# Cross-attention on one core: the key table's products first in slot 0, their rotation first on GpSimd, the mean row in slot 3

## The reference

```
kv_in = concatenate([context_hidden, draft_hidden], axis=1)      # 1601 + 256 rows per batch
q = rope(rms_norm((draft_hidden @ Wq.T) ...))                     # 16 heads of 128
k = rope(rms_norm((kv_in @ Wk.T) ...)); v = kv_in @ Wv.T          # 4 key heads, each used by 4 query heads
attn = softmax(q @ k.T * SCALE) @ v;  x = x + attn @ Wo.T
# for attention 1:
kv_c = kv @ W_kvc;  k_rope = rope(kv_c @ W_kr)                    # the "key table", 64 + 64 columns
# a query looks at the keys from its seg_id - 8 to its seg_id
```

## Time and profile before

| | us |
|---|---|
| three runs | 1948.34, 1949.68, 1951.16 (median 1949.68) |
| the profiled execution's own time | 1947.32 |
| its span | 1945.4 |
| span: TensorE matmul busy | 1723.2 (89%) |
| span: DVE / ACT / GpSimd busy | 1457.1 / 1087.0 / 1122.0 |

### The profile page before, as it was taken

How to read it: one execution, slowest core, us unless ns; L and a number is a source line. 1 busy time by engine, 2 the same in 40 slices (tenths; PEclk the granted TensorE clock), 3 DMA queues, 4 the chain that set the end, 5 groups by cost and what they waited for, 6 DMA issues and landing times. The chain is left out here.

```text
span 1945.4 us, 41606 instructions
## 1 busy us (share of the span) xinstructions
PE 1723.2 (89%) x14578; PEld 1314.0 (68%) x14727; DVE 1457.1 (75%) x3802; ACT 1087.0 (56%) x2676; POOL 1122.0 (58%) x1727
## 2 busy tenths in 40 slices
PE   4789898998998999999999899996999999089997
PEld 2578777787777777777778777775555555038974
DVE  7887896877978778788687787865757765675746
ACT  3567667676667666666766666663133333073543
POOL 5686686775857769568576685600256664072210
PEclk7899999999999999999999999996999999586998
DMA  4121110111110102101011100014368896510100
GB/s 137 46 75 40 34 33 12 40 64 37 50 35 9 34 8 95 43 12 44 1 38 49 54 22 12 8 51 185 117 209 269 270 268 191 161 31 16 45 11 26
DMA packets 74777, 140.25 MB, mean 72 GB/s; under 512 B 11177, under 2 KB 45970, under 8 KB 74322
## 3 DMA queue, kind: packets, MB, share of 16 engines
q1 hardware_dynamic: 64594, 107.21, 17.9%
q0 software_dynamic: 9984, 30.42, 4.4%
HBM read 111.73 MB, written 25.86 MB: 71 GB/s over the span
## 5 line engine op out<-in xcount | busy, mean ns | idle before, releaser
L897 DVE TENSOR_TENSOR att_pT<-att_pT 128x512 bf16<-128x512 f32 (+1 forms) x512 | 319.3, 649 | 156.8 <-ACT att_pT L764 153.6
L552 PE MATMUL att_out<-att_V,att_pT 128*128 128x128 bf16 x5760 | 390.8, 220 | 31.9 <-DVE att_pT L897 24.1
L552 PEld LDWEIGHTS att_out<-att_V,att_pT 128*128 128x128 bf16 x5760 | 351.1, 98 | 63.3 <-DVE att_pT L897 23.3
L764 ACT ACTIVATE att_pT<-att_pT 128x512 bf16<-128x512 f32 (+1 forms) x512 | 277.4, 569 | 172.4 <-PE att_pT L540 171.5
L770 ACT ACTIVATE att_prob<-att_scores,att_negmax 128x512 f32<-128x512 f32 (+1 forms) x512 | 330.1, 654 | 36.4 <-DVE att_negmax L886 34.8
L531 PE MATMUL att_scores<-att_K,att_Q 128*128 128x512 bf16 (+1 forms) x1408 | 299.1, 359 | 8.2 <-DVE att_K L859 1.4
L884 DVE TENSOR_REDUCE att_mx<-att_scores 128x1 f32<-128x512 f32 (+1 forms) x512 | 291.1, 628 | 0.6 <-PE att_scores L531 0.6
L540 PE MATMUL att_pT<-att_ident,att_prob 128*128 128x128 f32 x1920 | 276.5, 275 | 0.0
L531 PEld LDWEIGHTS att_scores<-att_K,att_Q 128*128 128x128 bf16 x1536 | 150.7, 98 | 145.3 <-issue 2.6
L453 PE MATMUL att_aux<-att_wkv,att_kvT 128*128 128x256 bf16 x1440 | 185.7, 280 | 36.9 <-DVE att_aT L859 16.3
L540 PEld LDWEIGHTS att_pT<-att_ident,att_prob 128*128 128x128 f32 x1920 | 210.6, 142 | 1.3
(11 more groups left out here) (329 smaller groups left out, 3176.6 us busy)
## 6 DMA issues: line engine op xcount, KB each, us to landing
moe_wa<-in_wa_l SPq DMA_DIRECT2D x80, 480.0 KB
att_wq<-wq_s SPq DMA_DIRECT2D x12, 512.0 KB, 5.3
att_wo<-wo_s SPq DMA_DIRECT2D x12, 512.0 KB, 6.3
moe_y<-y_s SPq DMA_DIRECT2D x8, 768.0 KB, 4.6
near_s<-att_stage POOLq DMA_DIRECT2D x8, 576.0 KB, 3.2
win_near<-near_s SPq DMA_DIRECT2D x32, 144.0 KB
moe_wb<-in_wb_l SPq DMA_DIRECT2D x80, 48.0 KB
att_cst<-in_ctx_l SPq DMA_DIRECT2D x6, 512.0 KB, 4.4
```

The lines of the kernel that those rows point to most:

```text
L552: last = nc.tensor.matmul(out_ps[:, i % 2, :], pT[:, i % 2, a, k, :], V[:, par, k, w, :], start=(k, a, w) == (0, 0, 0), stop=(k, a) == (KT ...
L764: nc.scalar.activation(pT[:, i % 2, 0, 4 * j:4 * j + m, :], pT_ps[j % 2][:, 0:m, :], ACT.Copy).then_inc(s["pt_hi"], 1)
L897: nc.vector.tensor_tensor(pT[:, i % 2, 1, 4 * j:4 * j + m, :], pT_ps[j % 2][:, 0:m, :], pT[:, i % 2, 0, 4 * j:4 * j + m, :], ALU.subtract) ...
```

## The change

The table `SLOTS` puts TB ahead in slot 0 (it was in slot 3), MN ahead in slot 3 (it was behind in slot 7). On DVE, the low part of a task ahead is taken within the four maxima, after the first bank in slot 5 and after the second elsewhere. The next batch's keys are split in slot 0 (in slot 2 in group 0 and in each fourth group), and summed two slots later. Angle steps go to slots 0, 3, 6 and 7, `turn_table` from slot 6 of the third group of a batch to slot 0 of the fourth. GpSimd rotates the table part first, corrects `stage` weights of slot 4 after all rotations, and gathers near rows at the end of a group; SP stores them. SP's order in a group begins with the table part.

```
@@ -93,14 +93,14 @@
 
 
 SLOTS = [
-    ([], [("KV", 0)], [("KV", 1)]),
+    ([("TB", 0)], [("KV", 0)], [("KV", 1)]),
     ([("AT-", 1)], [("KV", 2)], [("WO-", 1)]),
     ([("XT", 0)], [("Q", 0)], [("KV", 3)]),
-    ([("TB", 0)], [("Q", 1)], [("KV", 4)]),
+    ([("MN", 0)], [("Q", 1)], [("KV", 4)]),
     ([("KT", 0)], [("KV", 5)], [("KV", 6)]),
     ([("AT", 0)], [("KV", 7)], [("QT", 0)]),
     ([("KT", 1)], [("WO", 0)], [("QT", 1)]),
-    ([("KT", 2)], [("KT", 3)], [("MN", 0)]),
+    ([("KT", 2)], [("KT", 3)], []),
...
-PIECES_AT = {(0, 1): [(1, "O")], (0, 4): [(2, "K"), (2, "Q")], (1, 1): [(3, "K"), (3, "Q")], (1, 4): [(2, "O")], (2, 4): [(3, "O")]}
+PIECES_AT = {(0, 1): [(1, "O")], (0, 4): [(2, "K"), (2, "Q")], (1, 4): [(3, "K"), (3, "Q")], (2, 1): [(2, "O")], (2, 4): [(3, "O")]}
+NEAR_IN = [KVH * b + m for b in range(1, B) for m in range(2)]
+MEANS_IN = [1] + [KVH * b for b in range(1, B)]
+ANGLES_AT = {(0, 0): 0, (0, 3): 1, (0, 7): 2, (1, 3): 3, (1, 7): 4, (2, 0): 5, (2, 3): 6, (2, 6): 7, (2, 7): 8}
...
+def keys_slot(g):
+
+    return 2 if g == 0 or g % KVH == KVH - 1 else 0
...
+                def near_out(n):
+                    sp.wait_ge(s["gathered"], 16 * (n + 1))
+                    sp.dma_start(t["near_s"][n * P * WIN:(n + 1) * P * WIN, :].rearrange("(p j) c -> p (j c)", j=WIN), window).then_inc(s["stored"], 16)
...
+                    if g - 1 in NEAR_IN:
+                        near_out(NEAR_IN.index(g - 1))
+                    sp.wait_ge(s["tb_ready"], g + 1)
...
+                    if g + 1 < groups:
+                        turns_for(g + 1)
                     if g < SPLITS:
                         sp.wait_ge(s["c_sum"], g + 1)
                         next_keys(g + 1)
-                    for h, kind, after in ((2, "K", 3), (2, "Q", 3)) if g == 0 else ((2, "O", 7),) if g == 1 else ():
-                        sp.wait_ge(s["w_lo"], after)
-                        weight_in(h, kind)
                     if g == 0:
+                        sp.wait_ge(s["w_lo"], 3)
+                        weight_in(2, "K")
+                        weight_in(2, "Q")
                         weight_kept(1, "O")
...
+                    if i == 0 and not last and g < SPLITS and keys_slot(g) == 0:
+                        keys_high(g)
+                    if i == 0 and not last and g % KVH == KVH - 1 and g < (B - 1) * KVH:
+                        turn_table(g // KVH + 1)
...
-                    if i == 2 and g < SPLITS:
+                    if i == 2 and not last and g < SPLITS and keys_slot(g) == 2:
...
-                    if i == 6 and g % KVH == 2 and g < (B - 1) * KVH:
-                        turn_table(g // KVH + 1)
...
-                def row_max(tile, i):
+                def row_max(tile, i, ahead, g, u):
                     for k, (lo, n) in enumerate(BANKS):
+                        if k == (1 if i == 5 else 2):
+                            for x_ in ahead:
+                                task(*x_, g, u)
                         dve.wait_ge(s["qk_done"], NB * tile + k + 1)
                         nc.vector.reduce_max(mx[:, i % 2, k:k + 1], scores[:, lo:lo + n], AX.X).then_inc(s["bank_max"], 1)
...
-                    nc.vector.reduce_sum(sums[:, b, k, :], keys, AX.X).then_inc(s["c_sum"], 1)
+
+                def keys_sum(g):
+                    cols = key_columns(g % NB)
+                    nc.vector.reduce_sum(sums[:, g // NB + 1, g % NB, :], cst[:, :, 0:cols.stop - cols.start], AX.X).then_inc(s["c_sum"], 1)
...
                     if (g, i) == (0, 0):
+                        dve.wait_ge(s["wcat_hi"], 1)
+                        nc.vector.tensor_tensor(wcat[:, 1, :, :], wcat32[:, :, :], wcat[:, 0, :, :], ALU.subtract).then_inc(s["wcat_lo"], 1)
+                        weight_low_first("O")
                         for k in range(NB):
                             nc.vector.reduce_sum(sums[:, 0, k, :], first_part(k), AX.X).then_inc(s["first_sum"], 1)
-                        weight_low_first("O")
-                        dve.wait_ge(s["wcat_hi"], 1)
-                        nc.vector.tensor_tensor(wcat[:, 1, :, :], wcat32[:, :, :], wcat[:, 0, :, :], ALU.subtract).then_inc(s["wcat_lo"], 1)
...
-                        if i == 2:
+                        if i == keys_slot(g):
                             keys_low(g)
-                        if g % KVH == 1 and i == 0:
+                        if i == keys_slot(g) + 2:
+                            keys_sum(g)
+                        if g % KVH == 1 and i == 1:
                             normal_rows(b)
-                        if g % KVH == 1 and i >= 3:
-                            angle(b, i - 3)
-                        if g % KVH == 2 and 1 <= i <= 4:
-                            angle(b, i + 4)
+                        if (g % KVH, i) in ANGLES_AT:
+                            angle(b, ANGLES_AT[g % KVH, i])
...
                     now = g - 1
+                    turn_rows(now)
                     for order, (kind, n) in enumerate(POOL_ORDER):
                         rope(pool, order, kind, n, g, par)
                         if order == 2:
                             for h, k in PIECES_AT.get((now, 1), ()):
                                 weight_low(h, k)
-                        if order == 5:
-                            turn_rows(now)
-                            if now == 0:
-                                rstd(slice(2, TT), 2)
-                        if order == 7:
-                            for h, k in PIECES_AT.get((now, 4), ()):
-                                weight_low(h, k)
-                        if now >= KVH and now % KVH == 0:
-                            b = now // KVH - 1
-                            if order in (2, 6):
-                                gather(2 * b + order // 6)
-                            if order in (4, 8):
-                                store(2 * b + order // 8)
+                        if order == 5 and now == 0:
+                            rstd(slice(2, TT), 2)
+                    for h, k in PIECES_AT.get((now, 4), ()):
+                        weight_low(h, k)
+                    if now in NEAR_IN:
+                        gather(NEAR_IN.index(now))
```

More of the change, by code:

```diff
@@ L147, in tasks_of @@
         elif kind == "MN":
-            if g == 0 or (g % KVH == KVH - 1 and g < (B - 1) * KVH):
-                found.append((kind, (g + 1) // KVH, 0))
+            if g in MEANS_IN:
+                found.append((kind, MEANS_IN.index(g), 0))
         elif prep:
@@ L369, in _ @@
                 for g in range(groups):
+                    if g - 1 in NEAR_IN:
+                        near_out(NEAR_IN.index(g - 1))
+                    sp.wait_ge(s["tb_ready"], g + 1)
+                    b, k = divmod(g, NB)
+                    base = LOOKBACK + 512 * k
+                    if k < NB - 1:
+                        sp.dma_start(t[f"ktab_s{b}"][base:base + 512, :].rearrange("(j p) n -> p j n", p=P), trow[:, :, :]).then_inc(s["tb_out"], 16)
+                    else:
+                        sp.dma_start(t[f"ktab_s{b}"][base:base + CTX - 512 * k, :], trow[0:CTX - 512 * k, 0, :]).then_inc(s["tb_out"], 16)
+                    if g + 1 < groups:
+                        turns_for(g + 1)
                     if g < SPLITS:
@@ L392, in _ @@
                         sp.dma_start(wo[:, n % 2, :, :, :].rearrange("p a h n -> p (a h n)"), t["wo_s"][n % KVH].rearrange("p a n -> p (a n)")).then_inc(wo_load[n % 2], 16)
[L393 to L415 removed]
+                    if g in MEANS_IN:
+                        b = MEANS_IN.index(g)
                         sp.wait_ge(s["mean_ready"], b + 1)
                         sp.dma_start(t["mean_s"][b:b + 1, :], mean[:, :]).then_inc(s["mean_out"], 16)
+                    if g == 1:
+                        sp.wait_ge(s["w_lo"], 7)
+                        weight_in(2, "O")
+                        weight_kept(3, "K")
+                        weight_kept(3, "Q")
+                    if g == 2:
+                        sp.wait_ge(s["w_lo"], 9)
+                        weight_kept(3, "O")
+                for n in range(len(NEAR_IN), TT):
+                    near_out(n)
                 sp.wait_ge(s["tb_out"], 16 * groups)
@@ L990, in slot @@
                     if not last:
-                        row_max(tile, i)
-                    for x_ in ahead:
-                        task(*x_, g, u)
+                        row_max(tile, i, ahead, g, u)
+                    else:
+                        for x_ in ahead:
+                            task(*x_, g, u)
                     if old:
@@ L1124, in _ @@
                 turn_rows(groups - 1)
-                for n in (TT - 2, TT - 1):
+                for n in range(len(NEAR_IN), TT):
                     gather(n)
-                    store(n)
-                pool.wait_ge(s["stored"], 16 * TT)
 E_ALL, TOPK, GRP, TOP_GRP = 32, 6, 4, 2
```

38 lines of the change are left out of this document (10 added, 28 removed).

## The result

The changed kernel takes 1972.99 us (median of 4 runs, 1971.8 to 1978.44) against 1949.01 for the kernel before: ratio 1.013, interval [1.0106, 1.0153], slower by 24.0 us. The forecast was 1969 with a range of 1936 to 1989. The profiled execution has a span of 1971.0 us against 1945.4, 25.6 more; 1.1 of them lie before the first tile's maximum, 22.7 in groups 0 to 14, 2.2 in group 15, and -0.3 behind the attention.

What follows compares the result with a forecast made beforehand. TensorE was taken to set the pace, coupled in a ring with DVE and ACT. 31.5 - 26.0 + 13.6 = 19.1 us slower on 1947.3 gives 1966.4; with 2.4 for the median, 1969, range 1936 to 1989.

Steps and rivals of the forecast that it cites:

- part 1: Low parts inside the four maxima delay the first exponential: 2.1 us a group, 31.5 us slower over 15 groups.
- part 2: Extras of groups 1 to 12 (key split and sum, angle steps, gathers) mostly covered in new places: 26.0 us faster.
- plain group: Group 13, with no keys to split, angles or gathers: 75.4 us before, 77.5 forecast.
- part 3: First group: weights queued behind the keys stall ACT (10.7), clock 1.7, TB's late start 1.2: 13.6 us slower.
- KV7's wait: Slot 5: TensorE's 1.21 us for aT's low part, not returned because the values behind need quarter 2's low part.
- the addition ahead of QT1: Slot 6: DVE comes later to the addition to x right before QT1, with nothing covering it: 0.8 us a group.
- The page's 8 us: Table switches: by the skill page's drain of about 1.38 us, two switches a batch cost 2.8 us each time, 8 in all.
- (a): Reordering in the maxima is neutral, slots 5 to 7 giving back what 1 and 4 take: 1937.5 us, chance 0.13.
- (b): TensorE's waits in slots 5 to 7 all come back, 2.9 us a group gained: 1894 us, chance 0.08.
- (c): An in-between gain of 0.7 us a group from the maxima's reordering: 1948 us, same as before, chance 0.08.
- (d): No first-group stall, as keys and weights arrive before ACT reads them: 1957 us, chance 0.09.
- (e): Shifts add up to 3.4 us a group, or ACT pays more at table switches: 1988 us, chance 0.12.

Runs made afterwards that it cites:

- both half experiments: The kernel with both costs undone, low parts put back inside the maxima in slots 1 and 5 alone (1925.83 us), or 4, 6 and 7 alone (1935.43 us).
- the kernel with both costs undone: The changed kernel with low parts behind the maxima again and, in group 0, head 2's weights ahead of the keys in SP's queue: 1904.23 us.
- e4: The kernel before the change, with only the low parts moved inside the four maxima: 1975.45 us, ratio 1.0136.
- e1: The changed kernel with DVE taking the low parts of a slot's first task behind the four maxima again: 1911.92 us, ratio 0.9809.
- e2_weights_first: The changed kernel with SP issuing head 2's K and Q weights before it waits for the keys' sum in group 0: 1961.08 us.

## Why the prediction was right

The time was right (1969 against 1973), and the three steps happened where they were placed. The parts by the traces, in us:

| | forecast | measured |
|---|---|---|
| part 1, 15 groups | +31.5 | +35.6 |
| part 2, groups 1 to 12 above a plain group | -26.0 | -22.3 |
| part 3, group 0 above a plain group | +13.6 | +9.4 |
| group 15 | 0 | +2.2 |
| before and behind these | 0 | +0.8 |
| sum | +19.1 | +25.6 |

So the mechanisms were right in the main (but for what waits in group 0, below), and that the sum is closer than its parts is in some measure luck: part 3 was put too high by 4.2, while parts 1 and 2 came out dearer by 4.1 and 3.7 and group 15 added 2.2.

**Part 3, the first group: right in kind, too high in size.** The end of the sum was put at 121.1 (122.5) and the Q weights at 128.8 (taken at 129.71). What waits is not what was forecast, the values for DVE's low part, but the transposes ahead of them (L528), for ACT's scaled output that stands behind the same weights. Before the change these waited 0.25:

```profile
115.53 0.63 PE L508 MATMUL att_aux<-att_ident,att_attn 128*128 128x128 f32 x4 [0.25 <-ACT att_attn L776]
```

With the 2.59 of the values the slot's idle time grew from 2.84 to 13.32, by 10.5 for 10.7 forecast. The 1.7 added for the clock was wrong: the idle time of 13 us cost 0.3 more clock than that of 2.6. Stall and clock together are thus 10.8 for 12.4 forecast, and undoing the order gives 7.7 to 11.9. Moving the low half of TB's weights back returns 1.3 in the first tile (forecast for its late start 1.2). The group as a whole grew by only 9.4 beside part 1; where it gained the remaining 2.7 no run isolates.

**Part 1, the net figure right, the gross one too small.** From one block of scores to the next, the plain group changed against before by (us):

| slot | forecast | measured |
|---|---|---|
| 1 | 0.4 | 0.52 |
| 4 | 0.5 | 0.31 |
| 5 | 0.4 | 0.06 |
| 6 | 0.8 | 1.13 |
| 7 | 0 | 0.15 |

With 0.2 in slots 0 and 3 together, between which TB moved, that is 2.4 us a group for 2.1. The step on which it rests, that KV7's wait is not returned because the values need quarter 2, is shown by the rows and by both half experiments; so is the addition ahead of QT1. What was mis-sized is the term that was netted: I let the interleaving take back slot 7's 1.10 us for GpSimd and nothing more. By itself it costs 3.7 us a group (slot 6 1.64, slot 7 0.93), while the new place of GpSimd's rotation gives 1.3 back, in slots 6 (0.51) and 7 (0.79). Group 15 was left out of the sum, and lost 2.2.

**Part 2, right in place, mixed in size.** Forecast for this part, with the 1.10 of slot 7 in 15 groups and less 1.2 for TB: 26.0 + 16.5 - 1.2 = 41.3 us gained; the kernel with both costs undone gains 44.9. Groups 2, 6 and 10 are as long as the plain one (77.3, 77.8, 77.8), the split of the keys in slot 0 is covered (in none of its eight groups does DVE wait for the half of ACT), and 3, 7 and 11 are the longest but for the first. But these three keep 6.0 to 7.2 us over the plain group instead of 4.6. The term that is missing is the clock, which part 2 left out: without the 1.7 to 2.7 us that it costs there (an estimate, from the windows above), 4.3 to 4.5 are left, close to the forecast. Groups 4, 8 and 12 keep 1.2 instead of 0.1, and the second groups 0.2 instead of 1.7.

The Trainium skill, "ScalarE: Activation LUTs", section "What ACT_TABLE_LOAD costs", has a drain of about 1.38 us at a switch. Both switches above show none (320.42 to 321.71, 324.20 to 325.50); in the kernel after as in the one before the trace decides against it. The page's 8 us are not there.

**The rivals.** (a), (b) and (c) fell with e4 and e1: the interleaving is slower in either order, and nothing of KV7's wait comes back. (d) fell with ACT's 12.12 us. The side of (e) that lets shifts add up gave 3.4 us a group. The interleaving costs 3.7 by itself, but GpSimd's rotation gives 1.3 back, and 2.4 were measured.

## What to carry to other kernels

Where an engine's row of work sets the start of the next one (maximum, exponential, copy, low part), a task put inside that row can cost its own time and the wait for its input, even if it ends a wait further down (here 3.7 us a group, 1.5 at the end of the row): look for what the matmul behind that wait needs next. A queue that issues for several consumers in order (SP here) turns a harmless move of one producer into a stall of another, once in group 0 and twice again when the keys moved: for every moved signal, list all that the queue holds behind it. And parts are priced alone, in the order in which they will stand: the one edit cost 26 us in the old order and 57 to 61 in the new, where it and the stall hid 45 us of gain.

## What the runs showed of the hardware

I had not expected how far one DVE instruction's time depends on GpSimd. The same sum of squares of 128x128 takes 0.28 or 1.35 us, within one task of the changed kernel:

```profile
113.77 1.32 POOL L664 TENSOR_TENSOR att_scaled<-att_qraw,att_qw 128x512 f32<-128x512 f32 x1
...
113.89 1.35 DVE L899 SCALAR_TENSOR_TENSOR att_qjunk<-att_qraw 128x128 bf16<-128x128 f32 x1
...
115.17 1.42 POOL L666 TENSOR_TENSOR att_cosd<-att_scaled,att_tab 128x512 f32<-128x512 f32 x1
115.17 0.08 DVE L899 DVE_READ_ACCUMULATOR att_qjunk<-att_qraw 128x1 f32 x1
115.17 0.28 DVE L899 SCALAR_TENSOR_TENSOR att_qjunk<-att_qraw 128x128 bf16<-128x128 f32 x1
...
115.38 1.36 DVE L899 SCALAR_TENSOR_TENSOR att_qjunk<-att_qraw 128x128 bf16<-128x128 f32 x1
...
116.55 0.78 POOL L668 TENSOR_TENSOR att_sind<-att_scaled,att_tab 128x256 f32<-128x256 f32 x1
```

The long ones start up to 0.2 us behind the start of a product of GpSimd's and end some 0.15 us behind its end (the second, 115.38 + 1.36 = 116.74, behind 115.17 + 1.42 = 116.59); the short one starts together with one. Over the kernel with both costs undone, 113 of these 368 instructions start with no GpSimd arithmetic running, and all take 0.28 to 0.29 us; the 15 that start beside GpSimd's scaling of a query (L665 there) take 1.34 to 1.40. The Trainium skill, "SBUF — State Buffer", section "Terms", describes a port pair that DVE and GpSimd hold exclusively for a whole instruction; these numbers fit it. Others do not: the 33 squares that start while GpSimd takes the power of a handful of values (L679, 128x1 to 128x4, 0.6 to 1.2 us long) take 0.28 to 0.29 us as well, 23 of them wholly inside it. No run here moved one of the two engines to test either, so the cause stays open. It matters because the squares stand in DVE's full stretch from slot 4 to slot 6, where everything else in this case was decided.

The other surprise is the clock. Three kinds of TensorE's waits in groups 0 to 12 of the fourteen kernels, and how long it then worked at the lower level (half of that is lost):

| wait | cases | clock fell in | busy at the lower level (us) |
|---|---|---|---|
| 1.45 and 1.49 us, 0.9 us of work between (groups 3, 7, 11 with the sines in slot 0) | 30 | 20 | 2.7 to 5.9 |
| one of 2.0 to 3.6 us | 11 | 10 | 3.1 to 6.0 |
| one of 9.1 to 13.3 us | 4 | 4 | 2.9 to 5.6 |

So what a wait costs in clock does not grow with its length (1.7 us behind the idle 2.6 of the kernel before, 2.0 behind 13.3, 2.5 behind 3.6 in `e2_weights_first`), and the same two short waits cost nothing in one group and up to 3.0 us in another of the same program. A difference of that size between single groups of two traces is not to be explained by the change.
